# Router in three bf16 parts with rows turned by DMA on a relaxed schedule; shared rows loaded sooner; first gate and up product ahead of the last o product

## The reference, cut to what matters

```python
x = x + tanh(g_xattn) * attention(layernorm(x), ctx_512, Wq, w_kc_q, w_kc_kv, W_qr, W_kr, Wo)
x = x + tanh(g_ffn) * ffn(layernorm(x), router, w_up_gate, w_down, shared_w_up_gate, shared_w_down)
# ffn, on x_flat of 4096 rows of 512:
logits = einsum('td,de->te', x_flat, router)          # 8 experts
topk_logits, sel = top_k(logits, 2); cw = softmax(topk_logits)
# rows of an expert beyond its 1280 slots are dropped
y = routed(x_flat, sel, cw, w_up_gate, w_down) + down(silu(gate) * up)   # shared MLP of 1408
```

## Time and profile before

| | |
|---|---|
| median of three runs | 1960.39 us (1960.11 to 1962.2) |
| profiled execution | 1960.19 us, span 1958.4 us |
| busy in the span: PE, DVE, ACT, POOL | 1907.0, 947.1, 665.3, 603.6 us |
| granted TensorE clock, mean | 0.996 |
| attention loop, 134.76 to 758.25 us | PE busy 612.33 of 623.49 us |

### The profile page before, as it was taken

How to read it: one execution, slowest core, us unless ns; L and a number is a source line. 1 busy time by engine, 2 the same in 40 slices (tenths; PEclk the granted TensorE clock), 3 DMA queues, 4 the chain that set the end, 5 groups by cost and what they waited for, 6 DMA issues and landing times.

```text
span 1958.4 us, 32191 instructions
## 1 busy us (share of the span) xinstructions
PE 1907.0 (97%) x11972; PEld 1058.3 (54%) x11972; DVE 947.1 (48%) x1802; ACT 665.3 (34%) x1905; POOL 603.6 (31%) x651
## 2 busy tenths in 40 slices
PE   7799999999999999999999999999999999999999
PEld 7456666666656655444455555555544444444444
DVE  4776777776666666467332222222224424333233
ACT  5655556656655666320112222222210000000000
POOL 4644444444444455200213333433211111010101
PEclk9999999999999999999999999999999999999999
DMA  9444555654445655432269999999832532121202
GB/s 302 121 104 111 106 111 116 114 120 110 105 105 116 135 126 133 106 102 88 77 144 229 247 223 217 219 209 229 176 97 97 113 87 86 24 85 33 76 23 85
DMA packets 427299, 250.01 MB, mean 128 GB/s; under 512 B 360368, under 2 KB 366256, under 8 KB 427184
## 3 DMA queue, kind: packets, MB, share of 16 engines
q1 hardware_dynamic: 415664, 210.61, 46.2%
q0 software_dynamic: 11520, 37.76, 7.0%
HBM read 113.02 MB, written 48.23 MB: 82 GB/s over the span
## 4 chain that ended last, share of the span: by engine, by line
PE 58%; issue 13%; DVE 10%; POOL 8%; ACT 7%; DMA 2%; SPq 1%; DVEq 0%; POOLq 0%; ACTq 0%
PE score L725 11%; PE o L815 8%; PE score L804 7%; PE o L737 6%; PE p_bank L725 6%; PE m_bank L725 6%; DVE arena L1015 5%; ACT arena L892 4%; POOL arena L1385 4%; PE p_bank L804 4%; PE m_bank L804 4%; PE c_bank L737 3%; PE t_bank L737 3%; DVE arena L1097 2%; ACT arena L909 1%
## 5 line engine op out<-in xcount | busy, mean ns | idle before, releaser
L583 PE MATMUL o<-arena 128*128 128x512 bf16 x1536 | 352.3, 379 | 1.2 <-DVE arena L1015 1.2
L1015 DVE TENSOR_TENSOR arena<-arena 128x512 bf16<-128x512 f32 (+2 forms) x347 | 280.1, 814 | 74.1 <-ACT arena L845 58.0
L1385 POOL TENSOR_TENSOR arena<-arena 128x512 f32<-128x512 f32 x128 | 156.7, 1224 | 316.6 <-DVE arena L1036 314.8
L892 ACT ACTIVATE arena<-score,arena 128x128 f32<-128x128 f32 x512 | 181.6, 368 | 184.0 <-DVE arena L1097 183.9
L725 PE MATMUL score<-arena 128*128 128x512 bf16 x1056 | 235.1, 379 | 1.0 <-DMA arena<-xn_d 1.0
L583 PEld LDWEIGHTS o<-arena 128*128 128x128 bf16 x1536 | 150.3, 99 | 155.2 <-DVE arena L1015 1.7
L632 PE MATMUL p_bank<-arena 128*128 128x256 bf16 x1536 | 178.8, 273 | 0.3 <-DVE arena L1015 0.3
L725 PEld LDWEIGHTS score<-arena 128*128 128x128 bf16 x1056 | 103.2, 98 | 125.8 <-DMA arena<-xn_d 1.1
L815 PE MATMUL o<-arena 128*128 128x512 bf16 (+1 forms) x720 | 168.4, 379 | 0.6 <-DMA arena<-arena 0.6
L632 PEld LDWEIGHTS p_bank<-arena 128*128 128x128 bf16 x1536 | 145.3, 98 | 23.2 <-DVE arena L1015 0.5
L1471 POOL TENSOR_TENSOR arena<-arena 128x1088 bf16<-128x1088 f32 x32 | 71.9, 2246 | 274.2 <-ACT arena L922 274.2
(11 more groups left out here) (160 smaller groups left out, 2680.9 us busy)
## 6 DMA issues: line engine op xcount, KB each, us to landing
xrow_d<-arena SPq DMA_DIRECT2D x80, 256.0 KB, 3.7
arena<-w_expert SPq DMA_DIRECT2D x32, 544.0 KB, 5.3
arena<-w_shared SPq DMA_DIRECT2D x22, 384.0 KB, 3.4
arena<-x SPq DMA_DIRECT2D x16, 512.0 KB, 4.5
arena<-x SPq DMA_DIRECT2D x32, 256.0 KB, 3.4
x_d<-arena SPq DMA_DIRECT2D x32, 256.0 KB, 2.4
xn_d<-arena SPq DMA_DIRECT2D x32, 256.0 KB, 3.0
arena<-x_d SPq DMA_DIRECT2D x8, 1024.0 KB, 5.8
```

Of the source, the lines that this page charges most:

```text
L583: mm = pe.matmul(o_bank[b % 2][:, :], lhsT=cT[u % 2][:, a, h, :], rhs=M_w[:, w, head_of(hg, h), :], start=(hg == 0 and n == 0), stop=(hg = ...
L892: mm = act.activation(prob[:, u % 4, h, :], score_bank[u % 2][:, h * S:(h + 1) * S], ACT.Exp, bias=neg_max[:, u % 4, h:h + 1], accum_out=d ...
L1015: return dve.tensor_tensor(dst, src, hi, ALU.subtract)
L1385: pool.tensor_tensor(prob[:, u % 4], prob[:, u % 4], rden[:, u % 4, :].unsqueeze(2).broadcast_to([P, 4, S]), ALU.mult).then_inc(normed, 1)
```

## The change

The router's weights are split once into three bf16 parts (`router_w`, on VectorE ahead of the steps), and a batch's rows into three parts in `xn2_rows`: ScalarE casts the first, GpSimd subtracts it in place (`xn2_rest`), ScalarE casts the second (`xn2_mid`), GpSimd makes the third as a subtraction. The first two are stored as before. SyncE turns all three in one DMA transpose of twelve blocks (`turn_xn2`) into `xT2`, one buffer for the batches up to 30 and another for batch 31. TensorE multiplies in twelve matmuls of 24 columns, three weight parts side by side (`route`), and VectorE adds the three parts of 8 columns (`logits_of`). The identity matrix, the f32 transposes and their two copies on ScalarE fall away.

The steps: casts and subtractions of a batch go over steps 4 to 6; the transposes are issued in steps 6 and 0; the router stands at the end of steps 7 and 1, the sum of logits in steps 0 and 2. `ropeN` goes from step 4 to step 1. At the end `load_xs(0)` is spread over steps 118 to 121, `gate_up(0)` stands ahead of step 127, the routers of batches 30 and 31 after `gate_up(1)` and the first half of `gate_up(2)`, in the `o_bank`s, and two pieces of the shared weights are loaded sooner.

TensorE in the loop, before: steps 4 to 7 of a group (L632 and L636 are projections, L583 the o product, L596 shares by values, L610 scores, L670 transposes, L664 the router).

The diff, cut to its core:

```diff
+        router_sb = words(KT * E).rearrange("p (t e) -> p t e", t=KT)
+        router_w = halves(words(KT * 3 * E // 2)).rearrange("p (t w e) -> p t w e", t=KT, w=3)
...
-        xT32 = words(2 * D).rearrange("p (b n) -> p b n", b=2)
-        xn2_rows = [halves(words(D)).rearrange("p (l n) -> p l n", l=2) for _ in range(2)]
+        xn2_rows = [halves(words(3 * D // 2)).rearrange("p (l n) -> p l n", l=3) for _ in range(2)]
+        xT2_region = words(3 * D // 2)
+
+        def xT2(b):
+            region = xT2_region if b < NB - 1 else k_region[:, 5120:5888]
+            return halves(region).rearrange("p (l t n) -> p l t n", l=3, t=KT)
...
+                if m == 6:
+                    turn_xn2(2 * (k // 8 - 1), it)
+                if m == 0 and k // 8 - 2 < NG - 1:
+                    turn_xn2(2 * (k // 8 - 2) + 1, it)
...
+            def turn_xn2(b, it):
+                if within(b, NB):
+                    wait(sp, lg_mm, b if b < NB - 1 else 0, 4, it)
+                    if it is not None:
+                        sp.sem_inc(turn_begun, 1)
+                    sp.dma_start_transpose(xT2(b).rearrange("p l t n -> p (l t) n"),
+                                           xn2_rows[b % 2].rearrange("p l n -> p (l n)")).then_inc(xT2_in[b % 2], 16)
...
-            run_steps(sp, step, NU - 2)
-            sp.wait_ge(scored, NU // 2)
+            run_steps(sp, step, XS_STEP - 1)
+            sp.wait_ge(scored, NU // 2 - 4)
+            sp.wait_ge(pr_mm, 8 * NG)
             for p in range(2):
                 sp.wait_ge(xn2_out[p], 16 * 2)
-            load_xs(0, None)
-            for k in range(NU - 1, LAST_STEP + 1):
+            for k in range(XS_STEP, LAST_STEP + 1):
                 step(k, None)
+                if k < XS_STEP + 4:
+                    load_xs(0, None, [k - XS_STEP])
+            sp.wait_ge(ct_mm, NU)
+            turn_xn2(NB - 1, None)
+            load_wsh(12)
+            load_wsh(13)
...
-                m = k % 8
                 c = k // 8
-                if m in (4, 5):
-                    b = 2 * (c - 1) + m - 4
-                    if within(b, NB):
-                        wait(pe, xn2_ready, b + 1, 4, it)
-                        misc_free(b, 2 * (c - 1), it)
-                        ln_transposes(xn2[:, b % 2, :], l2_mm)
-                if m in (6, 7):
-                    b = 2 * (c - 1) + m - 6
-                    if within(b, NB):
-                        wait(pe, l2_up, b + 1, 4, it)
-                        misc_free(2 * c, b, it)
-                        for t in range(KT):
-                            mm = pe.matmul(m_bank[:, 0:E], lhsT=xT32[:, b % 2, t * P:(t + 1) * P],
-                                           rhs=router_sb[:, t * E:(t + 1) * E], start=(t == 0), stop=(t == KT - 1))
-                        mm.then_inc(lg_mm, 1)
-
-            def ln_transposes(rows, done):
-                for t in range(KT):
-                    mm = pe.transpose(m_bank[:, t * P:(t + 1) * P], rows[:, t * P:(t + 1) * P], ident_sb)
-                mm.then_inc(done, 1)
+                if k % 8 in (7, 1):
+                    b = 2 * (c - 1) if k % 8 == 7 else 2 * c - 3
+                    if within(b, NB - 2):
+                        wait(pe, lg_up, b, 4, it)
+                        route(b, m_bank, it)
+
+            def route(b, bank, it):
+                wait(pe, xT2_in[b % 2], 16 * (b // 2 + 1), 32, it)
+                if b == 0:
+                    pe.wait_ge(router_split, 5)
+                for n in range(3 * KT):
+                    mm = pe.matmul(bank[:, 0:3 * E], lhsT=xT2(b)[:, n // KT, n % KT, :],
+                                   rhs=router_w[:, n % KT].rearrange("p w e -> p (w e)"),
+                                   start=(n == 0), stop=(n == 3 * KT - 1))
+                mm.then_inc(lg_mm, 1)
...
-            for k in range(-12, NU):
+            for k in range(-12, NU - 1):
                 step(k, None)
             gate_up(0, None)
-            for k in range(NU, LAST_STEP - 2):
+            step(NU - 1, None)
+            for k in range(NU, LAST_STEP + 1):
                 step(k, None)
-            gate_up(1, None, (0,))
-            step(LAST_STEP - 2, None)
+            pe.wait_ge(lg_up, NB - 2)
+            gate_up(1, None)
+            gate_up(2, None, (0,))
             pe.wait_ge(x1_done, NB)
+            for b in (NB - 2, NB - 1):
+                route(b, o_bank[b % 2], None)
+            pe.wait_ge(lg_up, NB)
             down(0, None)
...
+                if m in (5, 6):
+                    b = 2 * (c - 1) + m - 5
+                    if within(b, NB):
+                        wait(act, xn2_rest, b + 1, 4, it)
+                        act.copy(xn2_rows[b % 2][:, 1, :], xn2[:, b % 2, :]).then_inc(xn2_mid, 1)
+                if m in (4, 5):
+                    b = 2 * (c - 1) + m - 4
+                    if within(b, NB):
+                        wait(act, xn2_ready, b + 1, 4, it)
+                        wait(act, xn2_out[b % 2], 16 * (b // 2), 32, it)
+                        wait(act, xT2_in[b % 2], 16 * (b // 2), 32, it)
+                        act.copy(xn2_rows[b % 2][:, HI, :], xn2[:, b % 2, :]).then_inc(xn2_hi, 1)
...
+            def logits_of(b, bank, it):
+                wait(dve, lg_mm, b + 1, 4, it)
+                parts = bank[:, 0:3 * E].rearrange("p (w e) -> p e w", w=3)
+                dve.tensor_reduce(logits[:, b, :] if it is None else logits[:, bass.ds(at(b, 4, it), 1), :],
+                                  parts if it is None else parts.unsqueeze(1), AX.X, ALU.add).then_inc(lg_up, 1)
...
+                        wait(pool, xn2_mid, b + 1, 4, it)
+                        pool.tensor_tensor(xn2_rows[b % 2][:, 2, :], xn2[:, b % 2, :], xn2_rows[b % 2][:, 1, :],
+                                           ALU.subtract).then_inc(xn2_lo, 1)
                 if m in (4, 5):
                     b = 2 * (c - 1) + m - 4
                     if within(b, NB):
                         wait(pool, xn2_hi, b + 1, 4, it)
-                        pool.tensor_tensor(xn2_rows[b % 2][:, LO, :], xn2[:, b % 2, :], xn2_rows[b % 2][:, HI, :],
-                                           ALU.subtract).then_inc(xn2_lo, 1)
+                        pool.tensor_tensor(xn2[:, b % 2, :], xn2[:, b % 2, :], xn2_rows[b % 2][:, HI, :],
+                                           ALU.subtract).then_inc(xn2_rest, 1)
...
-                if m == 4 and within((k + 4) // 8, NG):
-                    g = (k + 4) // 8
+                if m == 1 and within((k + 7) // 8, NG):
+                    g = (k + 7) // 8
```

73 lines of the change are left out of this document (32 added, 41 removed).

## The result

The changed kernel takes 1943.36 us (median of four runs, 1942.95 to 1946.03) against 1960.33 us of the kernel before beside it: a ratio of 0.9913 with a 95% interval from 0.9899 to 0.9927. That is faster by 0.9%, more than the 0.2% that a measurement of this kernel can tell. The profiled execution took 1942.95 us, its span is 1941.1 against 1958.4.

What follows compares the result with a forecast made beforehand. TensorE's own instruction list plus small waits was taken as the bound in the loop. 1960.2 - 20 (loop) - 4 (last steps) + 4 (turn) - 1 (start) = 1939 us; forecast range 1932 to 1948, chance 0.56.

Steps and rivals of the forecast that it cites:

- A, the loop: The 13.5 groups of eight steps, 134.76 to 758.25 us: 1.49 us less a group, a gain of 20 us.
- Rival 2: In the loop, the moved table product takes back the whole gain: 1959 to 1960 us; chance 0.14 for 1948 to 1962.
- Rival 1: In the loop, VectorE is clear of the table product: gain 31 us, time about 1929; chance 0.22.
- Rival 3: In the loop, turned rows come late and TensorE waits, 3.5 us a group: 1986 us; chance 0.06 for 1965 and more.
- the signs: Group 44 to 45.5 us; step 3 wait 1.0 to 1.6, VectorE; no step 6 GpSimd wait; matmuls 40 to 55 ns.
- B: The last steps before the last o product, 758.25 to 804.69 us: a gain of 4 us (0 to 6).
- C: The turn to the feed-forward part: a loss of 4 us (0 to 8).
- The single file: Behind the last o product the last routers come one after another; the first down product starts at about E + 20 us.
- E: The end of the last o product, from which the times at the turn were counted.
- D: The start: the first product with values no longer waits 1.24 us for the table product; 1 us gained.
- the delay d: Table product at step 1 slows VectorE, lengthening the wait of step 3: 0.8 us a group, 0 to about 2.3.

Runs made afterwards that it cites:

- route_twice: The changed kernel with every router product run twice, 24 matmuls of 128x24 for a batch instead of 12: 1946.65 us, ratio 0.9932 to the kernel before.
- rope_m3: The changed kernel with GpSimd's table product for the values at step 3 of a group instead of step 1: 1932.77 us, ratio 0.9856 to the kernel before.
- rope_m4: The changed kernel with the table product for the values put back to step 4: 1958.20 us, ratio 0.9996 to the kernel before.
- own29: The changed kernel with a separate buffer for the turned rows of batch 29: 1944.74 us, ratio 0.9924 to the kernel before.
- o_first: The changed kernel with the first gate and up product behind the last o product again: 1940.89 us, ratio 0.9897 to the kernel before.
- rope_m3_cast: rope_m3 with ScalarE's two casts of the next rows in step 2 moved behind the value product's cast: 1922.20 us, ratio 0.9806 to the kernel before.

## Why the prediction came out as it did

The time, 1943 against a forecast of 1939, lies in the range, the direction is right and so is the largest term. But the working of that term was wrong in one step, and that it came out near is luck: two of its errors met.

**A, the loop: 16.4 us won, 20 forecast.** The failed step is "One batch's twelve stand at the end of step 7, where nothing waits: 0.55 us paid", together with the 1.64 us of f32 passes counted as won in full. I took the chain that step 3 waits for to begin at step 1 or 2, since the rows I had read ended there. It begins with the scores of step 6, and both router products lie inside it. So of 2 x (0.82 - 0.30) us saved there nothing came off the time; `route_twice` shows that the router products could as well be doubled. What did come off is what lies outside the chain. The transposes of two batches, 0.44 us each, make 0.88 a group. The wait at step 6, which I took by its label at 0.32, is 0.48 by the distance that I used at step 3: the product starts 448.57 - 445.50 = 3.07 us after the o product ahead of it, where 443.76 - 441.17 = 2.59 is usual. The chain itself grew by 0.13 (30.09 to 30.22). Together that is 1.23, and the group fell from 46.18 to 607.12 / 13.5 = 44.97, by 1.21. In the sum 1.64 - 0.55 = 1.09 us stood as won and never was, and the 0.8 us of delay stood as lost and was made good elsewhere; that these nearly cancel made the term look right.

The mis-sized terms were smaller: the router's twelve matmuls take 0.30 us, not 0.55. The delay by the table product at step 1 is 0.89 us by `rope_m3` (30.22 against 29.33), close to the 0.8 taken and far from the upper end of 2.3, as only two links were held up at length. The Trainium skill, page "SBUF — State Buffer", section "SBUF: two separate sides", says that the loser at the shared port pair is blocked for the whole of the other's instruction; the two links that end with GpSimd's operation, 0.58 and 0.52 us instead of 0.16, fit that. But the same product had cost the chain about as much at step 4 in the kernel before, by holding up the share product and with it the row maximum of step 6: it starts 451.80 - 449.31 = 2.49 us after the scores there, and 1.33 in the changed kernel and with the move alone. The whole way is 30.09 us there and 30.18 with the move alone. I had priced that end of the move only at its visible wait of 0.32. The move is neutral for the chain, and without it the subtractions added to GpSimd would have eaten the gain (`rope_m4`).

Rival 2, that a longer chain takes back the loop's gain, was nearer to the mechanism than the forecast: the chain gave nothing, but it hardly grew either. Rival 1 (1929) would have needed the chain to be free of the table product, and that is `rope_m3`, 1932.8. Rival 3, turned rows late in the loop, did not occur: no wait of the router in the loop before 740. (Its price was low by its own numbers: 10.5 less 8 us is 2.5 at step 1 and not 2.)

Of the signs, the group, the missing wait at step 6 and the name of VectorE at step 3 came as written. The wait of step 3 grew to 1.71 us, past the 1.6 written, the router's matmuls took 25 ns each instead of 40 to 55, and TensorE stood still for some 6 us at the turn instead of 10.

**B: 2.0 us, 4 forecast**, inside its bounds. The waits that I put at VectorE and ScalarE are there, 1.8 us in three, and two of 1.7 and 1.6 us for turned rows, which I had not listed for these steps.

**C: 1.6 us lost, 4 forecast.** The single file is there nearly as worked out: E is 791.73 + 2.59 = 794.32, and the first down product starts 18.5 us later, 20 forecast. The cause that I gave for its first part was wrong in half: of the buffer and the x1 store, it is the store (`own29`). That the products put ahead make the file start later, and that `o_first` therefore starts the first down product 5.2 us sooner, I had not seen; but the time gained little from it.

**D: 0.2 us lost, 1 won forecast.** The 1.24 us wait for GpSimd at the start is gone, and at 110.57 us TensorE is 0.7 us ahead of the kernel before. The key projection of step 3 then starts 0.2 us later than before, at 112.93, since its wait for VectorE is 1.55 us there instead of 0.63: the delay d again, already ahead of the loop.

## What to carry over

A wait of half a microsecond before one instruction can be the visible end of a chain that holds many steps: before work is taken off the engine that looks like the bound, measure the distance between two waits on it, and if another engine's instructions fill that whole distance, only work outside it counts. Here two edits to the order of GpSimd and ScalarE did as much as the whole change, and only with the chain shortened did TensorE's shorter list show. When an operation is moved, price both its old and its new place by what queues behind it, not by the wait that carries its name.

## What the runs showed of the hardware

- Twelve matmuls of 128x24, each with its own weights of 128x128, hold TensorE for 0.30 us, 25 ns each; the nearest shapes of the kernel before took 39 and 54 ns.
- A VectorE operation on four elements a row took 0.58 us instead of 0.16 beside a GpSimd operation of 0.73 us, and ended within 0.04 us of that one's end (step 1 of the changed kernel against `rope_m3`).
- After a standstill of 4.86 us TensorE ran 3.4 us at a granted clock of 0.50 and part of the next 3.4; after one of 2.21 us in `o_first` it ran 2.6 us at 0.50. After the waits of 1.5 to 1.8 us in the loop the clock stayed at 1.00, and in `o_first` also after one of 3.26 us at 803.87, while in `rope_m3_cast` one of 1.95 us at 748.50 was followed by an o product of 4.44 us instead of 2.75. So the length of a standstill alone did not tell here whether the clock fell.
